# Key/value weights in two transfers, and another order for the first tiles of a cross-attention and expert layer

## The chip, the cores and the metric

One core of a Trainium2 chip runs the whole kernel. The metric is the device time of one execution in microseconds, the median of several; lower is better. The engines are PE (TensorE, the matrix engine; PEld is its weight load), DVE (VectorE), ACT (ScalarE), POOL (GpSimd) and SP (SyncE, which here only issues transfers).

## The reference

The input `x` is (16, 64, 512): 1024 tokens of width 512. `ctx` has the same shape. One block of cross attention with 32 query heads and 8 key/value heads of width 16, then a gated low-rank expert layer:

```python
x = x + _L0_xattn_ref(_layernorm(x), ctx_4096, ctx_4096, itok_BxS2_0_2047, Wq, Wk, Wv, Wo)
x = x + _L0_ffn_ref(_layernorm(x), A_w, B_w, Wq_w, keys)
...
q, k, v = heads(query @ Wq), heads(key @ Wk), heads(value @ Wv)
q = q * cos + _rotate_half(q) * sin
k = k * cos + _rotate_half(k) * sin
probs = softmax(q @ k.T * scale)
out = (probs @ v) @ Wo
...
scores = (x @ Wq_w.T) @ keys.T
top_vals, top_idx = top_k(scores, 16)
gate = one_hot(top_idx) weighted by softmax(top_vals)
out = ((x @ A_w.T) * gate) @ B_w.T * SCALING
```

## The kernel before

The 1024 tokens are cut into 8 tiles of 128 (two batches of 64 each). Every engine has a program of its own, written out by hand: a function `first()`, a function `second()`, then `step(i)` for i from 1 to 5, and `last()`. Semaphores with counts order the engines against each other. No scheduler decides anything: the order of the work on an engine is the order of the calls.

Products are made in reduced-precision pairs. A float32 operand `w` is split into a high part `w_hi` (ACT, `split_hi`, a rounded copy) and a low part `w_lo` (`split_lo`, `w - w_hi`); a product is then hi*hi + hi*lo + lo*hi. In the listing `high_part` makes the first two and `low_part` the third. The first tiles are an exception: `raw_kv(0)`, `raw_kv(1)` and `raw_q(0)` multiply the float32 operands as they are, since the split weights are not ready then.

What the change touches lies in the first 25 us:

- **SP** issues the loads, first tile 0 of `x`, then `wkv` (the key and value weights, 512 KB), the four quarters of `wq`, and so on. ACT issues tile 0 of the context (`cT_in`, 256 KB) from its own queue.
- **PE** begins with `keep_warm`: 11 products of zeros (`WARM`), started as soon as DVE has cleared their operand. Then come `raw_kv(0, [0, 1])`, the transposes of the normalised tile 0 (`turn_xh(0)`), `raw_kv(0, [2, 3])`, four `raw_q(0, k)`, `raw_kv(1)`, `turn_xh(1)`, `turn_q(0)` (transposes of the rotated queries of tile 0), four small products of the router weights (`ROUTE`), the first half of tile 1's query projection, `scores(0, b)`, `turn_k(1)`, the other half of the projection, `turn_xh(2)`, `kv_high(2)`, `turn_m(0)`, `kv_low(2)`, and then `second()`, which begins with `turned_scores(0)`.
- **ACT** rounds the weights (`wkv_hi`, `wq_hi`), copies the transposed tile 0 (`xT_raw`), makes the sine and cosine tables `cs`, normalises tile 1 (`xh`, `normalise(1)`) and rounds the transposed results (`xT_hi`, `qT_hi`).
- **POOL** makes the low parts `wkv_lo` and `wq_lo` (line L311), and the standard deviations: `deviation1(t)` writes `rstd` and `shift`, which ACT's `normalise(t)` waits for.
- **DVE** rotates queries and keys, makes the low parts `xT_lo`, `qT_lo`, `kT_lo` of what comes out of PSUM, and the maxima of the scores (`top`, line L856), from which `m_parts` makes `m_split` for `turn_m`. In `attend(t)` it normalises the attention's output, which ACT rounds (`oT_hi`) for PE's `out_high(t)`.

`scores(0, 0)` waits for `qT_hi`, `qT_lo`, the blocks of keys and the router's copy; `turn_xh(1)` waits for `xh`; `turn_m(0)` waits for `m_split`.

Of the kernel before, what the change touches and what calls it, by code (L numbers as in the profile page):

```python
# [15 lines left out]
DK = D // P  # L16
# [27 lines left out]
WARM = 11  # L44
# [10 lines left out]
def build(nc, x, xT, cT, pos, wq, wqT, wkv, wo, aT, router, bT, out):  # L55
    ctx = ExitStack()
    with ctx:
# [6 lines left out]
        def sem(name):  # L64
            return ctx.enter_context(nc.semaphore(name))
# [136 lines left out]
        ld_wkv = sem("ld_wkv")  # L202
# [7 lines left out]
        wq_h, wq_l, wkv_h, wkv_l = sem("wq_h"), sem("wq_l"), sem("wkv_h"), sem("wkv_l")  # L210
# [27 lines left out]
        def _(sp):  # L238
# [29 lines left out]
            sp.dma_start(wkv_sb[:], wkv).then_inc(ld_wkv, 16)  # L268
# [39 lines left out]
        def _(pool):  # L308
            def split_lo(lo, raw, hi, high, low, k):
                pool.wait_ge(high, k + 1)  # L310
                pool.tensor_tensor(lo[:, k, :], raw[:, k, :], hi[:, k, :].bitcast(F32),  # L311
                                   ALU.subtract).then_inc(low, 1)
# [95 lines left out]
            def first():  # L408
                deviation1(0)
                pool.wait_ge(rope_step, 9)  # L410
                for k in range(DK):
                    split_lo(wkv_lo, wkv_sb, wkv_hi, wkv_h, wkv_l, k)
                split_lo(wq_lo, wq_sb, wq_hi, wq_h, wq_l, 0)
                deviation1(1)
                split_lo(wq_lo, wq_sb, wq_hi, wq_h, wq_l, 1)
                k_blocks(0, 0)
                k_blocks(0, 1)
                split_lo(wq_lo, wq_sb, wq_hi, wq_h, wq_l, 2)
                split_lo(wq_lo, wq_sb, wq_hi, wq_h, wq_l, 3)
# [61 lines left out]
        def _(act):  # L481
# [145 lines left out]
            def first():  # L627
                act.wait_ge(const_ok, J + 1)
                act.activation(preload[:, 0:1], half_pi[:], ACT.Sin)
                act.wait_ge(ld_wkv, 16)  # L630
                for k in range(DK):
                    split_hi(wkv_hi, wkv_sb, wkv_h, k)
# [137 lines left out]
        def _(dve):  # L770
# [220 lines left out]
            def first():  # L991
# [38 lines left out]
                                pick_sum[:].unsqueeze(3).broadcast_to([P, 2, 2, BATCH])).then_inc(sel_ok, 1)  # L1030
                dve.wait_ge(cs_ok, 4)
                rotate_k(0)
                statistics1(1)
                k_low(0)
# [4 lines left out]
                                  table(HD, 0, H), ALU.mult).then_inc(q_rot, 1)  # L1039
                dve.wait_ge(q_rot, 1)  # L1040
# [94 lines left out]
        def _(pe):  # L1135
# [33 lines left out]
            def kv_high(t):  # L1169
                if t == RAW:  # L1170
                    pe.wait_ge(wkv_l, DK)
                    pe.wait_ge(v_st_ok, t)
                pe.wait_ge(c_hi_ok, t - RAW + 1)
                high_part(ps_w1[:, 0:2 * KV], chunk(cT_hi), wkv_hi, wkv_lo, slice(0, 2 * KV))
# [161 lines left out]
            def first():  # L1336
# [3 lines left out]
                pe.wait_ge(ld_wkv, 16)  # L1340
                raw_kv(0, [0, 1])
                turn_xh(0)
                raw_kv(0, [2, 3]).then_inc(kv_ps, 1)
                for k in range(DK):
                    pe.wait_ge(ld_wq[k], 16)
                    mm = raw_q(0, k)
                    if k == 2:
                        turn_k(0)
                mm.then_inc(q_ps, 1)
                raw_kv(1).then_inc(kv_ps, 1)  # L1350
                pe.wait_ge(kT_lo_ok, 1)
                turn_xh(1)
                turn_q(0)
# [4 lines left out]
                mm.then_inc(route_ps, 1)  # L1358
                q_high_part(1, [0, 1])
                q_low_part(1, [0, 1])  # L1360
# [3 lines left out]
                turn_k(1)  # L1364
                project_q(1, [2, 3]).then_inc(q_ps, 1)
                pe.wait_ge(qT_lo_ok, 1)
                turn_xh(2)
                kv_high(2)
                turn_m(0)
                kv_low(2)  # L1370

            def second():
                pe.wait_ge(sel_ok, 2)
                turned_scores(0)
                pe.wait_ge(q_rot, 4)
# [177 lines left out]
```

## Time and profile before

| | |
|---|---|
| median of 3 runs | 171.19 us (170.63 to 171.31) |
| the profiled execution | 170.7 us |
| its span on the core | 169.0 us |
| PE busy | 163.9 us, 97% |
| DVE busy | 132.8 us, 79% |
| ACT, POOL busy | 90.1 us, 91.8 us |

The span runs from the first to the last recorded instruction; the 1.7 us beside it are the launch and the end. Positions below are microseconds from the span's start. A busy time on PE contains the stretches in which one product drains while the next is fed, so consecutive rows of PE overlap; what a piece of work costs PE is the distance between the starts of its first row and of the next piece's.

### The profile page before, as it was taken

What the parts mean: (1) busy time and instruction counts of PE and PEld (TensorE: products, weight loads), DVE (VectorE), ACT (ScalarE), POOL (GpSimd) and SP (SyncE); (2) the same over time, 40 slices, a digit from 0 to 9 for tenths busy, and PEclk for the clock granted to TensorE, in tenths of its full rate; (3) what the DMA queues carried; (4) which work ended last, traced back from release to release, by engine and by line L of the source; (5) the groups of instructions that cost most, each with busy time, mean ns of one, the idle gap of its engine ahead of it and who ended that gap; (6) DMA issues with size and microseconds to landing.
All of it is one profiled execution on the core that took longest, in us unless ns stands there. A gap on an engine that the chain in (4) does not pass through costs nothing.

```text
span 169.0 us, 4082 instructions
## 1 busy us (share of the span) xinstructions
PE 163.9 (97%) x1439; PEld 130.2 (77%) x1439; DVE 132.8 (79%) x393; ACT 90.1 (53%) x212; POOL 91.8 (54%) x114
## 2 busy tenths in 40 slices
PE   7999999999999999999999999999999999999993
PEld 2647786777878787888879787888879776889883
DVE  2849896996998899669995799669985988767752
ACT  3397889899656462733635462733338154333210
POOL 5489989999899654830493354930450303512100
PEclk9999999999999999999999999999999999999999
DMA  5899980403203020301003000100001001000013
GB/s 170 306 418 385 407 260 10 124 31 100 66 0 124 4 62 0 113 16 62 6 0 124 0 4 0 62 6 0 4 0 62 4 0 62 8 0 0 0 62 124
DMA packets 6595, 13.46 MB, mean 80 GB/s; under 512 B 816, under 2 KB 1200, under 8 KB 6320
## 3 DMA queue, kind: packets, MB, share of 16 engines
q1 hardware_dynamic: 6288, 12.95, 21.9%
q8 instruction: 11, 0.18, 0.5%
q10 hardware_dynamic: 288, 0.27, 0.5%
q14 instruction: 8, 0.07, 0.1%
HBM read 11.11 MB, written 2.10 MB: 78 GB/s over the span
## 4 chain that ended last, share of the span: by engine, by line
PE 83%; DVE 7%; ACT 6%; issue 2%; ACTq 0%; DVEq 0%
PE ps_w L1145 14%; PE ps_w L1146 13%; PE ps_w L1150 12%; PE ps_t L1158 7%; PE ps_s L1230 6%; PE ps_s L1266 5%; PE ps_s L1249 4%; PE ps_w L1138 3%; PE ps_w L1140 3%; PE ps_t L1163 3%; PE ps_w L1139 3%; ACT eT L567 2%; PE ps_s L1146 2%; PE ps_s L1150 2%; PE ps_s L1145 2%
## 5 line engine op out<-in xcount | busy, mean ns | idle before, releaser
L364 POOL TENSOR_TENSOR oT_lo<-o_n,oT_hi 128x512 fp32r<-128x512 f32 x8 | 10.3, 1289 | 27.0 <-ACT oT_hi L575 26.9
L856 DVE TENSOR_REDUCE ps_s<-ps_s 128x8 f32<-128x512 f32 x32 | 21.0, 691 | 0.8 <-PE ps_s L1230 0.6
L567 ACT ACTIVATE eT<-ps_s 128x512 f32<-128x512 f32 x32 | 17.0, 600 | 4.6 <-PE ps_s L1255 4.5
L379 POOL TENSOR_TENSOR late<-late,gate 128x512 f32<-128x512 f32 x7 | 7.6, 1080 | 15.2 <-DVE gate L949 15.2
L1145 PE MATMUL ps_w<-am_hi,x2T_hi 128*128 128x288 f32 x48 | 14.0, 313 | 0.0
L355 POOL TENSOR_TENSOR k_bd_lo<-kT_lo,half_mask 128x512 fp32r<-128x512 f32 x8 | 8.3, 1041 | 10.3 <-DVE kT_lo L820 10.3
L1146 PE MATMUL ps_w<-am_lo,x2T_hi 128*128 128x288 f32 x48 | 13.1, 295 | 0.0
L874 DVE STREAM_TRANSPOSE o_s<-ps_s 128x1024 f32<-128x1024 f32 x8 | 10.0, 1244 | 2.2 <-PE ps_s L1266 2.2
L1145 PE MATMUL ps_w<-wo_hi,oT_hi 128*128 128x512 f32 x28 | 11.3, 404 | 0.3 <-ACT oT_hi L575 0.3
L1138 PE MATMUL ps_w<-wq_hi,xT_hi 128*128 128x512 f32 x26 | 11.2, 429 | 0.0
L575 ACT ACTIVATE oT_hi<-o_n 128x512 fp32r<-128x512 f32 x8 | 5.1, 631 | 11.4 <-DVE o_n L889 11.4
L1146 PE MATMUL ps_w<-wo_lo,oT_hi 128*128 128x512 f32 x28 | 11.0, 394 | 0.0
L1145 PE MATMUL ps_w<-b_hi,zT_hi 128*128 128x512 f32 (+1 forms) x28 | 10.8, 390 | 0.0
L1145 PEld LDWEIGHTS ps_w<-am_hi,x2T_hi 128*128 128x128 f32 x48 | 9.0, 188 | 1.9 <-ACT late L599 0.5
L560 ACT ACTIVATE mT<-ps_s 128x256 fp32r<-128x256 f32 x8 | 3.1, 383 | 13.8 <-PE ps_s L1239 13.8
L1146 PE MATMUL ps_w<-b_lo,zT_hi 128*128 128x512 f32 (+1 forms) x28 | 10.4, 377 | 0.0
L917 DVE TENSOR_TENSOR x2T_lo<-ps_t,x2T_hi 128x512 fp32r<-128x512 f32 x7 | 4.8, 690 | 7.0 <-ACT x2T_hi L588 7.0
L1140 PE MATMUL ps_w<-wq_hi,xT_lo 128*128 128x512 f32 x26 | 10.3, 394 | 0.0
L1139 PE MATMUL ps_w<-wq_lo,xT_hi 128*128 128x512 f32 x26 | 10.2, 392 | 0.0
L1230 PE MATMUL ps_s<-k_bd_hi,qT_hi 64*128 64x256 f32 x64 | 10.1, 310 | 0.0
L345 POOL TENSOR_TENSOR q_r<-q_a,q_b 128x512 f32<-128x512 f32 x7 | 9.1, 1297 | 0.5 <-DVE q_b L839 0.5
L1230 PE MATMUL ps_s<-k_bd_hi,qT_lo 64*128 64x256 f32 x64 | 9.2, 279 | 0.0
(236 smaller groups left out, 530.4 us busy)
## 6 DMA issues: line engine op xcount, KB each, us to landing
x_sb<-x SPq DMA_DIRECT2D x8, 256.0 KB, 7.1
cT_in<-cT SPq DMA_DIRECT2D x7, 256.0 KB, 3.3
out<-res SPq DMA_DIRECT2D x7, 256.0 KB, 2.0
wq_sb<-wq SPq DMA_DIRECT2D x4, 256.0 KB, 6.5
late<-wo SPq DMA_DIRECT2D x1, 1024.0 KB, 9.0
am_sb<-aT SPq DMA_DIRECT2D x1, 1024.0 KB, 8.7
b_sb<-bT SPq DMA_DIRECT2D x1, 1024.0 KB, 7.1
xT_raw<-xT SPq DMA_DIRECT2D x4, 256.0 KB, 3.0
```

The costliest lines, as they stand in the source:

```text
L364: pool.tensor_tensor(oT_lo[:], o_n[:].rearrange("p (b r q) -> p r b q", b=2, r=REP), oT_hi[:].bitcast(F32), ALU.subtract).then_inc(oT_lo_o ...
L567: act.activation(eT[:, c].rearrange("p b n -> p (b n)"), ps_s[:, c, :], ACT.Exp)\
L856: dve.tensor_reduce(neg_top[:, b, HALF_H * half:HALF_H * (half + 1), :], ps_s[:, 2 * (1 - b) + half, :].rearrange("p (r h k) -> p h r k", ...
L874: dve.transpose(o_s[:].rearrange("p h u g d -> p (h u g d)"), ps_o.rearrange("p h n -> p (h n)")).then_inc(o_step, 1)
L1138: pe.matmul(dst, hi(k), w_hi[:, k, cols], start=(k == 0), stop=False)
L1139: pe.matmul(dst, hi(k), w_lo[:, k, cols], start=False, stop=False)
L1140: mm = pe.matmul(dst, lo(k), w_hi[:, k, cols], start=False, stop=(k == DK - 1))
L1145: pe.matmul(dst, hi(k), w_hi[:, k, cols], start=(k == 0), stop=False)
L1146: pe.matmul(dst, hi(k), w_lo[:, k, cols], start=False, stop=False)
L1150: mm = pe.matmul(dst, lo(k), w_hi[:, k, cols], start=False, stop=(k == DK - 1))
L1158: mm = pe.transpose(dst[:, P * k:P * (k + 1)], src[:, P * k:P * (k + 1)], ident[:])
L1230: mm = pe.matmul(ps_s[:, 2 * (1 - b) + half, 2 * P * rp:2 * P * (rp + 1)], q[rows, t % 2, b, 2 * rp:2 * rp + 2, :].rearrange("p r q -> p ( ...
```

## The change

`wkv` is loaded in two transfers of 256 KB, each with its semaphore, and PE begins `raw_kv(0, [0, 1])` when the first half is there. `WARM` goes from 11 to 9. The low parts of the last two quarters of `wkv` are made by DVE and no longer by POOL. On PE `turn_k(0)`, `turn_q(0)`, `q_low_part(1)`, `turn_m(0)` and `kv_low(2)` move; on DVE `k_low(0)` moves behind the first half of the rotation of tile 0's queries; on POOL the second quarter of `wq_lo` moves ahead of `deviation1(1)`.

```diff
@@ -41,7 +41,7 @@
 SCALE = float(HD) ** -0.5
 GATE_SCALE = 32 / TOP
 STEPS = 12
-WARM = 11
+WARM = 9
 TAKEN = -3.0e38
 MAGIC = 1.5 * 2.0 ** 23
 TWO_PI = 2 * np.pi
@@ -199,7 +199,7 @@
         ld_c = [sem(f"ld_c{t}") for t in range(T)]
         ld_wq = [sem(f"ld_wq{k}") for k in range(DK)]
         ld_xT = {t: sem(f"ld_xT{t}") for t in range(DIRECT, T)}
-        ld_wkv = sem("ld_wkv")
+        ld_wkv = [sem(f"ld_wkv{half}") for half in range(2)]
         wq_sum_ok, sums_ps, sums_ok = (sem(n) for n in ("wq_sum_ok", "sums_ps", "sums_ok"))
         ld_wqT = [sem(f"ld_wqT{k}") for k in range(DK)]
         cs_q_ok, q_mean_ok = sem("cs_q_ok"), sem("q_mean_ok")
@@ -207,7 +207,7 @@
         sel_ok, const_ok, mask_step = sem("sel_ok"), sem("const_ok"), sem("mask_step")
         v_ones = sem("v_ones")
         rope_step, cs_ok = sem("rope_step"), sem("cs_ok")
-        wq_h, wq_l, wkv_h, wkv_l = sem("wq_h"), sem("wq_l"), sem("wkv_h"), sem("wkv_l")
+        wq_h, wq_l, wkv_h, wkv_l, wkv_l_late = (sem(n) for n in ("wq_h", "wq_l", "wkv_h", "wkv_l", "wkv_l_late"))
         wo_h, wo_l, am_h, am_l, b_h, b_l = (sem(n) for n in ("wo_h", "wo_l", "am_h", "am_l", "b_h", "b_l"))
         route_ps, route_ok = sem("route_ps"), sem("route_ok")
         stat1, rstd1_ok, shift1_ok = sem("stat1"), sem("rstd1_ok"), sem("shift1_ok")
@@ -265,7 +265,9 @@
                 sp.dma_start(out[t], res[:]).then_inc(stored, 16)
 
             load_x(0)
-            sp.dma_start(wkv_sb[:], wkv).then_inc(ld_wkv, 16)
+            for half in range(2):
+                ks = slice(2 * half, 2 * half + 2)
+                sp.dma_start(wkv_sb[:, ks, :], wkv[:, ks, :]).then_inc(ld_wkv[half], 16)
             for k in range(DK):
                 sp.dma_start(wq_sb[:, k, :], wq[:, k, :]).then_inc(ld_wq[k], 16)
             load_x(1)
@@ -408,11 +410,11 @@
             def first():
                 deviation1(0)
                 pool.wait_ge(rope_step, 9)
-                for k in range(DK):
+                for k in range(2):
                     split_lo(wkv_lo, wkv_sb, wkv_hi, wkv_h, wkv_l, k)
                 split_lo(wq_lo, wq_sb, wq_hi, wq_h, wq_l, 0)
+                split_lo(wq_lo, wq_sb, wq_hi, wq_h, wq_l, 1)
                 deviation1(1)
-                split_lo(wq_lo, wq_sb, wq_hi, wq_h, wq_l, 1)
                 k_blocks(0, 0)
                 k_blocks(0, 1)
                 split_lo(wq_lo, wq_sb, wq_hi, wq_h, wq_l, 2)
@@ -627,8 +629,8 @@
             def first():
                 act.wait_ge(const_ok, J + 1)
                 act.activation(preload[:, 0:1], half_pi[:], ACT.Sin)
-                act.wait_ge(ld_wkv, 16)
                 for k in range(DK):
+                    act.wait_ge(ld_wkv[k // 2], 16)
                     split_hi(wkv_hi, wkv_sb, wkv_h, k)
                 x_raw(0)
                 act.wait_ge(rope_step, 9)
@@ -1028,15 +1030,17 @@
                 dve.wait_ge(sel_ok, 1)
                 dve.tensor_copy(sel[:].rearrange("p b (h k) -> p b h k", h=2),
                                 pick_sum[:].unsqueeze(3).broadcast_to([P, 2, 2, BATCH])).then_inc(sel_ok, 1)
+                split_lo(wkv_lo, wkv_sb, wkv_hi, wkv_h, wkv_l_late, 2)
+                split_lo(wkv_lo, wkv_sb, wkv_hi, wkv_h, wkv_l_late, 3)
                 dve.wait_ge(cs_ok, 4)
                 rotate_k(0)
                 statistics1(1)
-                k_low(0)
                 dve.wait_ge(q_ps, 1)
                 H = REP * KVH
                 w = ps_w0[:].rearrange("p (h s j) -> p h s j", h=H, s=2)
                 dve.tensor_tensor(q_b[:].rearrange("p (h s j) -> p h s j", h=H, s=2), w[:, :, ::-1, :],
                                   table(HD, 0, H), ALU.mult).then_inc(q_rot, 1)
+                k_low(0)
                 dve.wait_ge(q_rot, 1)
                 dve.tensor_tensor(w, w, table(0, 0, H), ALU.mult).then_inc(q_rot, 1)
                 dve.wait_ge(q_rot, 2)
@@ -1168,7 +1172,8 @@
 
             def kv_high(t):
                 if t == RAW:
-                    pe.wait_ge(wkv_l, DK)
+                    pe.wait_ge(wkv_l, 2)
+                    pe.wait_ge(wkv_l_late, 2)
                     pe.wait_ge(v_st_ok, t)
                 pe.wait_ge(c_hi_ok, t - RAW + 1)
                 high_part(ps_w1[:, 0:2 * KV], chunk(cT_hi), wkv_hi, wkv_lo, slice(0, 2 * KV))
@@ -1337,41 +1342,41 @@
                 pe.wait_ge(warm_ok, 1)
                 keep_warm(ps_t1[:], WARM)
                 pe.wait_ge(ident_ok, 1)
-                pe.wait_ge(ld_wkv, 16)
+                pe.wait_ge(ld_wkv[0], 16)
                 raw_kv(0, [0, 1])
                 turn_xh(0)
+                pe.wait_ge(ld_wkv[1], 16)
                 raw_kv(0, [2, 3]).then_inc(kv_ps, 1)
                 for k in range(DK):
                     pe.wait_ge(ld_wq[k], 16)
                     mm = raw_q(0, k)
-                    if k == 2:
-                        turn_k(0)
                 mm.then_inc(q_ps, 1)
+                turn_k(0)
                 raw_kv(1).then_inc(kv_ps, 1)
                 pe.wait_ge(kT_lo_ok, 1)
                 turn_xh(1)
-                turn_q(0)
                 pe.wait_ge(ld_router, 16)
                 for k in range(DK):
                     rows = slice(QUAD * k, QUAD * (k + 1))
                     mm = pe.matmul(ROUTE[:, k, :], router_sb[rows, 0:P], router_sb[rows, P:P + E], start=True, stop=True)
                 mm.then_inc(route_ps, 1)
+                turn_q(0)
                 q_high_part(1, [0, 1])
-                q_low_part(1, [0, 1])
                 pe.wait_ge(route_ok, 1)
                 scores(0, 0)
                 scores(0, 1)
                 turn_k(1)
+                q_low_part(1, [0, 1])
                 project_q(1, [2, 3]).then_inc(q_ps, 1)
                 pe.wait_ge(qT_lo_ok, 1)
                 turn_xh(2)
+                turn_m(0)
                 kv_high(2)
-                turn_m(0)
-                kv_low(2)
 
             def second():
                 pe.wait_ge(sel_ok, 2)
                 turned_scores(0)
+                kv_low(2)
                 pe.wait_ge(q_rot, 4)
                 project_q(2, [0, 1])
                 turn_q(1)
```

PE, from the raw query products of tile 0 (`wq_sb,xT_raw`) to the query projection of tile 1 (`wq_hi`, `wq_lo`; `eT` holds the router weights here). Before:

```order
L1334 MATMUL ps_w<-wq_sb,xT_raw 128x512 x3
L1186 MATMUL ps_t<-ident,k_r 128x128
L1334 MATMUL ps_w<-wq_sb,xT_raw 128x512
L1328 MATMUL ps_w<-wkv_sb,cT_in 128x256 x4
L1158 MATMUL ps_t<-ident,xh 128x128 x4
L1158 MATMUL ps_t<-ident,q_r 128x128 x4
L1357 MATMUL ps_s<-eT 128x64 x4
L1145 MATMUL ps_w<-wq_hi,xT_hi 128x512
L1146 MATMUL ps_w<-wq_lo,xT_hi 128x512
L1145 MATMUL ps_w<-wq_hi,xT_hi 128x512
L1146 MATMUL ps_w<-wq_lo,xT_hi 128x512
L1150 MATMUL ps_w<-wq_hi,xT_lo 128x512 x2
```

And in the changed kernel (its lines are numbered 4 or 5 higher):

```order
L1339 MATMUL ps_w<-wq_sb,xT_raw 128x512 x4
L1191 MATMUL ps_t<-ident,k_r 128x128
L1333 MATMUL ps_w<-wkv_sb,cT_in 128x256 x4
L1162 MATMUL ps_t<-ident,xh 128x128 x4
L1361 MATMUL ps_s<-eT 128x64 x4
L1162 MATMUL ps_t<-ident,q_r 128x128 x4
L1149 MATMUL ps_w<-wq_hi,xT_hi 128x512
L1150 MATMUL ps_w<-wq_lo,xT_hi 128x512
L1149 MATMUL ps_w<-wq_hi,xT_hi 128x512
L1150 MATMUL ps_w<-wq_lo,xT_hi 128x512
L1235 MATMUL ps_s<-k_bd_hi,qT_hi 128x256 x2
```

The transpose of the rotated keys (`k_r`) has gone from the midst of the query products to behind them, the router's products ahead of the transposes of `q_r`, and the row with `xT_lo` no longer stands ahead of the scores.

PE, around the transposes of the maxima (`m_split`) of tile 0. Before, the last products of `kv_high(2)` and `kv_low(2)` stand on both sides of them:

```order
L1146 MATMUL ps_w<-wkv_lo,cT_hi 128x256
L1145 MATMUL ps_w<-wkv_hi,cT_hi 128x256
L1146 MATMUL ps_w<-wkv_lo,cT_hi 128x256
L1239 MATMUL ps_s<-ident,m_split 128x128 x2
L1150 MATMUL ps_w<-wkv_hi,cT_lo 128x256 x4
L1249 MATMUL ps_s<-qT_hi,k_bd_hi 128x256 x4
L1249 MATMUL ps_s<-qT_hi,k_bd_lo 128x256 x4
L1249 MATMUL ps_s<-qT_lo,k_bd_hi 128x256 x4
```

In the changed kernel the transposes follow `turn_xh(2)` at once:

```order
L1144 MATMUL ps_w<-wq_hi,xT_lo 128x512
L1162 MATMUL ps_t<-ident,xh 128x128 x4
L1244 MATMUL ps_s<-ident,m_split 128x128 x2
L1149 MATMUL ps_w<-wkv_hi,cT_hi 128x256
L1150 MATMUL ps_w<-wkv_lo,cT_hi 128x256
```

and `kv_low(2)` (the row with `cT_lo`) stands behind the whole of `turned_scores(0)`:

```order
L1254 MATMUL ps_s<-qT_hi,k_bd_lo 128x256 x4
L1254 MATMUL ps_s<-qT_lo,k_bd_hi 128x256 x4
L1260 MATMUL ps_s<-mT,sel 128x256 x4
L1154 MATMUL ps_w<-wkv_hi,cT_lo 128x256 x4
L1142 MATMUL ps_w<-wq_hi,xT_hi 128x512
```

So the maxima are wanted eight products earlier, and the four of `kv_low(2)` come later.

POOL, from `deviation1(0)` to the first block of keys. Before:

```order
L320 TENSOR_TENSOR rstd<-ve,neg_half 128x1
L311 TENSOR_TENSOR wkv_lo<-wkv_sb,wkv_hi 128x256 x4
L311 TENSOR_TENSOR wq_lo<-wq_sb,wq_hi 128x512
L320 TENSOR_TENSOR rstd<-ve,neg_half 128x1
L327 TENSOR_SCALAR shift<-mv,rstd 128x1
L311 TENSOR_TENSOR wq_lo<-wq_sb,wq_hi 128x512
L355 TENSOR_TENSOR k_bd_hi<-kT_hi,half_mask 128x512
```

And in the changed kernel:

```order
L322 TENSOR_TENSOR rstd<-ve,neg_half 128x1
L313 TENSOR_TENSOR wkv_lo<-wkv_sb,wkv_hi 128x256 x2
L313 TENSOR_TENSOR wq_lo<-wq_sb,wq_hi 128x512 x2
L322 TENSOR_TENSOR rstd<-ve,neg_half 128x1
L329 TENSOR_SCALAR shift<-mv,rstd 128x1
L357 TENSOR_TENSOR k_bd_hi<-kT_hi,half_mask 128x512
L357 TENSOR_TENSOR k_bd_lo<-kT_lo,half_mask 128x512
```

Two of the four `wkv_lo` are gone, and both `wq_lo` stand ahead of `rstd` and `shift` of tile 1.

## Rows read from the trace of the kernel before

**Rows 1.** The page of the kernel before: busy shares, and the chain by engine.
```profile
PE 163.9 (97%) x1439; PEld 130.2 (77%) x1439; DVE 132.8 (79%) x393; ACT 90.1 (53%) x212; POOL 91.8 (54%) x114
...
PE 83%; DVE 7%; ACT 6%; issue 2%; ACTq 0%; DVEq 0%
```

**Rows 2.** Busy time by stretch; columns PE, PEld, DVE, ACT, POOL, clock, DMA, GB/s.
```profile
1.24:6.00 4.76, 4.76 (x11) 1.51 (x12) 2.24 (x10) 1.83 (x4) 2.35 (x12) 1.00 0.80 260
6.00:7.53 1.53, 1.53 (x5) 1.25 (x5) 1.39 (x7) 0.99 (x4) 0.52 (x1) 1.00 0.82 270
...
7.97:8.91 0.94, 0.94 (x6) 0.60 (x5) 0.00 (x0) 0.74 (x3) 0.94 (x2) 1.00 1.05 405
31.71:47.93 16.22, 16.06 (x150) 12.21 (x150) 14.07 (x34) 13.65 (x36) 15.05 (x14) 1.00 0.28 77
```

**Rows 3.** DMA issues of the first 6 us: KB each, us from issue to landing.
```profile
wkv_sb<-wkv SPq DMA_DIRECT2D x1, 512.0 KB, 4.4
cT_in<-cT ACTq DMA_DIRECT2D x1, 256.0 KB, 4.6
```

**Rows 4.** When the two transfers were issued: start us, us, queue, line.
```profile
1.22 0.46 ACTq L483 DMA_DIRECT2D cT_in<-cT  x1
...
1.24 0.42 SPq L268 DMA_DIRECT2D wkv_sb<-wkv  x1
```

**Rows 5.** POOL's timeline: start us, us, line, tiles, [idle before, releaser].
```profile
7.01 2.83 POOL L311 TENSOR_TENSOR wkv_lo<-wkv_sb,wkv_hi 128x256 fp32r<-128x256 f32 x4 [1.64 <-ACT wkv_hi L486]
10.13 1.28 POOL L311 TENSOR_TENSOR wq_lo<-wq_sb,wq_hi 128x512 fp32r<-128x512 f32 x1 [0.29 <-ACT wq_hi L486]
11.74 0.56 POOL L320 TENSOR_TENSOR rstd<-ve,neg_half 128x1 f32<-128x1 f32 x1 [0.33 <-DVE ve L787]
12.40 0.27 POOL L327 TENSOR_SCALAR shift<-mv,rstd 128x1 f32<-128x1 f32 x1
```

**Rows 6.** ACT's timeline.
```profile
12.85 0.80 ACT L498 ACTIVATE xh<-x_sb,shift,rstd 128x512 f32<-128x512 f32 x1
...
14.89 0.60 ACT L509 ACTIVATE xT_hi<-ps_t 128x512 fp32r<-128x512 f32 x1 [0.72 <-PE ps_t L1158]
15.63 0.60 ACT L552 ACTIVATE qT_hi<-ps_t 128x512 fp32r<-128x512 f32 x1
```

**Rows 7.** PE's timeline.
```profile
14.26 0.60 PE L1158 MATMUL ps_t<-ident,xh 128*128 128x128 f32 x4
14.94 0.66 PE L1158 MATMUL ps_t<-ident,q_r 128*128 128x128 f32 x4
...
15.90 0.51 PE L1145 MATMUL ps_w<-wq_hi,xT_hi 128*128 128x512 f32 x1
...
17.51 0.39 PE L1230 MATMUL ps_s<-k_bd_hi,qT_hi 64*128 64x256 f32 x2
...
19.12 0.33 PE L1186 MATMUL ps_t<-ident,k_r 128*128 128x128 f32 x1
...
20.68 0.60 PE L1158 MATMUL ps_t<-ident,xh 128*128 128x128 f32 x4
...
25.66 0.60 PE L1158 MATMUL ps_t<-ident,q_r 128*128 128x128 f32 x4
...
31.71 0.47 PE L1145 MATMUL ps_w<-wo_hi,oT_hi 128*128 128x512 f32 x1 [0.33 <-ACT oT_hi L575]
```

**Rows 8.** DVE's timeline.
```profile
9.56 0.30 DVE L807 TENSOR_TENSOR ps_w<-ps_w,cs 128x128 f32<-128x128 f32 x1 [1.67 <-ACT cs L638]
...
16.26 0.69 DVE L844 TENSOR_TENSOR qT_lo<-ps_t,qT_hi 128x512 fp32r<-128x512 f32 x1
...
18.52 2.63 DVE L856 TENSOR_REDUCE ps_s<-ps_s 128x8 f32<-128x512 f32 x4 [0.57 <-PE ps_s L1230]
...
21.51 0.29 DVE L868 TENSOR_TENSOR m_split<-ps_s,m_split 128x128 fp32r<-128x128 f32 x1
...
26.98 0.69 DVE L844 TENSOR_TENSOR qT_lo<-ps_t,qT_hi 128x512 fp32r<-128x512 f32 x1 [1.46 <-ACT qT_hi L552]
```

## The prediction, made before the changed kernel had run

> **What bounds the kernel now.** I read the page first. PE is busy for 97% of the span, and the chain that ended last lies on PE for 83% [rows 1]. So only two kinds of change can move the time: work taken off PE, and waits of PE taken away or added. The change removes two products of zeros and no useful product, so everything goes by waits. The windows show where they are: from 31.71 to 47.93 PE is busy for 16.06 of 16.22 us [rows 2], and it stays like that up to the last stages. What counts is therefore how early PE reaches 31.71 us. Its timeline names what held it there: `out_high(0)` waited 0.33 us for `oT_hi` [rows 7], the end of `attend(0)` on DVE, and DVE begins that chain with `qT_lo` of tile 1 at 26.98, after 1.46 us idle for `qT_hi` [rows 8], which needs PE's `turn_q(1)` at 25.66 [rows 7]. So `turn_q(1)` is the point to follow: if it moves by d, everything behind it moves by d. PE does the same useful work before it in both kernels. Only its start, its waits and its clock differ.
>
> **The start.** Eleven products of zeros end near 6.0 [rows 2], 0.43 us each. The first product needs context tile 0, which lands at 1.22 + 4.6 = 5.8, and `wkv`, at 1.24 + 4.4 = 5.6 [rows 3, 4]. With nine, PE is free at about 5.1. The halved load has 256 KB less in front of or beside the context; at the 380 GB/s or so that the engines move when full (405 in one window [rows 2]) that is 0.65 us, a landing at 5.15, and with at most the 0.2 us from landing to product that the trace has, a start at 5.4. The bounds are 5.1 (free PE) and 6.0 (nothing gained). I take 5.4: 0.6 us earlier.
>
> Half of that is lost to the clock. The first two chunks took 1.53 us, the last two, the same work, 0.94 [rows 2]. The zeros, 512 columns in 0.43 us, ran at the level of 1.2 GHz, the last two chunks at 2.4; wholly at the lower level the first two would take twice 0.94, less the short wait in it, 1.8. So the clock rose near 7.2, inside the first product, though the profile's clock column prints 1.00 throughout. Begun at 5.4, that product runs at the lower level to its end: 5.4 + 1.8 = 7.2 against 7.53. The gain is **-0.3 us**.
>
> The second half of `wkv` lands where the whole did, about 5.7 to 5.9, and is wanted at 7.7: at nothing. ACT rounds those quarters 0.3 us later than now and waits for `xh`'s transposes anyway.
>
> **To the transposes of tile 1.** From 8.91 to 14.26 PE works without a wait: 5.35 us. From 8.6 that ends at 13.95. But `xh` of tile 1 is late now. POOL starts the first `wq_lo` at 10.13, when ACT has rounded its quarter, and took the rest in the order `rstd`, `shift`, `wq_lo` [rows 5]. ACT's rounding follows PE, so 9.83. Now both `wq_lo` come first: 9.83 + 2 x 1.28 = 12.35; `rstd` and `shift` took 12.67 - 11.74 = 0.93, so `shift` is ready at 13.3 instead of 12.67. ACT starts `xh` at 13.3, not 12.85, and takes 0.80 [rows 6]: PE can start at 14.12. That is **+0.15 us** of waiting. The two `wkv_lo` taken off POOL (0.71 each [rows 5]) help nothing, because POOL then waits for ACT's `wq_hi`: it would have been idle.
>
> On DVE the two `wkv_lo` cost between 0.30 (128x128) and 0.69 us (128x512) each [rows 8]: 0.6 to 1.4 in the 1.67 us in which DVE waited for the tables `cs` [rows 8]. At nothing; if that cover went, at most the excess over 1.67 would reach `rotate_k(0)`.
>
> **To the scores.** In the trace the four transposes (0.44, from 7.53 to 7.97 [rows 2]) ended at 14.70 and `turn_q(0)` began at 14.94 [rows 7]: 0.24 us wait for `q_r`. In the new order the router's products, about 0.4 of the 0.96 from 14.94 to 15.90 [rows 7], fill it: 14.12 + 0.44 + 0.4 = 14.96. The wait goes, **-0.24**, but `turn_q(0)` is where it was. So `qT_hi` (15.63 [rows 6]) and `qT_lo` (16.26 + 0.69 = 16.95 [rows 8]) are where they were. `k_low(0)`, about 0.3 us, now stands inside the rotation, but the query product ends 0.4 earlier (start, and `turn_k` behind it): `q_r` is ready at 14.7, under cover of the router.
>
> The scores need `qT_lo`: 17.0 at the earliest. The six products from 15.90 to 17.51 took 1.61 us [rows 7], the two low ones a third, 0.54. PE starts the four at 15.5 and is done at 16.6. `q_low_part`, which now covers that time, stands behind the scores. So PE waits **+0.4 us** for DVE. That is where the reordering gives back what it won: PE reaches the scores 0.5 us earlier and has 0.54 us of work still to do.
>
> **To `turn_q(1)`.** Scores 17.0 to 18.6 (1.61, from 17.51 to 19.12), then `turn_k(1)`, the low part and the rest, 1.56 + 0.54 [rows 7]: `turn_xh(2)` at 20.7, as now (20.68). Then comes `turn_m(0)`, at 21.15 if free. DVE begins `top` 1.01 us after the scores began (18.52 - 17.51) and has `m_split` 3.28 later (21.51 + 0.29 - 18.52 [rows 8]): 17.0 + 1.0 + 3.3 = 21.3. Before, `kv_high(2)` stood in front and covered this. **+0.15 to 0.2 us**. Behind it the same products come in another order up to `turn_q(1)`; I take 0.1 us off for a short wait on `mT` and a change of operand kind that the order saves (an estimate; the trace has both at about 0.1).
>
> **The sum at `turn_q(1)`:** -0.3 + 0.15 - 0.24 + 0.4 + 0.2 - 0.1 = +0.1 us. The values of tile 0 and the projection behind start some tenths earlier or later, but PE then waits longer at 31.71 for the same DVE chain. The rest costs nothing: the fifth context load waits for `kv_low(2)`, which ends a good microsecond later, but its buffer is read many microseconds on; SP's one issue more (0.42 us [rows 4]) delays transfers that the full DMA engines (share 1.05 [rows 2]) would have held back anyway. So 170.7 + 0.1 = 170.8 in terms of the profiled execution, which lies 0.5 us under the median of the runs shown, 171.2. **Predicted: 171.3 us.** A measurement of this kernel tells about 0.5%, 0.86 us, from no change.
>
> **A rule against the change.** 256 KB and 512 KB both move at about the full rate here [rows 2, 3], so splitting costs no bandwidth. "DMA: Bandwidth & Descriptors" of the Trainium skill, "Rules for kernel authors", says that two transfers of disjoint halves are not worth it, since they use the same engines, and wants 1 MiB in each. Its example is halves by partition; taken over, it is the first rival.
>
> **Rivals.**
>
> 1. *The split gains nothing*: context tile 0 still lands at 5.8, the product starts at 6.0, PE idles 0.9 us behind the nine products. For it: the same bytes go through the same engines. Against it: half of `wkv` moves behind the context. The -0.3 goes: 171.2 + 0.4 = 171.6. Chance 0.13.
> 2. *The waits don't come*: `qT_lo` or `m_split` is ready sooner, because DVE and ACT gain the 0.3 of the start too. Without the 0.4 and 0.2, 170.7. If in addition the clock rises before the first product in most executions, its start gives the whole 0.6 and `xh` follows: 171.3 - 0.6 - 0.3 = 170.4, and a few tenths more would be faster by over 0.5%. Chances 0.12 and 0.06.
> 3. *The clock rises late, slower*: PE is now idle from 5.1 to 5.4, shortly ahead of the point at which the clock rose, where it had been busy since 1.24. If the rise then took as long from 5.4 as it took from 1.24, it would come at 11.4; 4.2 us of work at half the clock cost 2.1 us, of which the waits for `xh` and `qT_lo` absorb some 0.4: 173.0. It decides (0.86 us over 171.2) if the rise is later than about 9.5. Against it: 0.3 us is short beside the 3.9 us of work ahead of it and the products behind it. Chance 0.09. "TensorE: Matmul & The Clock Gate" of the Trainium skill, "What's actually happening", says that the throttled state is the default, that activity releases it, and that the point varies from run to run; no run here shows yet what a short gap does.
>
> **How the numbers follow.** The forecast has 0.60; it spans 170.9 to 171.7, by 0.3 to 0.4 either way for the landing and the clock. The two cases near it inside 0.5% have 0.25. Same: 0.85. Faster: 0.06. Slower: 0.09. The range takes in rivals 1 and the first of 2 and the spread of the runs shown (0.7 us): 170.5 to 172.0.
>
> **What would show each step.** PE's first product at 5.3 to 5.5 and its first transposes near 7.2. DVE's `wkv_lo` near 0.4 us each, done before `cs`. ACT's `xh` of tile 1 at 13.3. `turn_q(0)` within 0.15 of 14.94, and no wait before it. A wait of PE of 0.3 to 0.5 us for `qT_lo` before the scores, and one of 0.1 to 0.3 for `m_split`. `turn_q(1)` at 25.6 to 25.9, `out_high(0)` at 31.7 to 31.9, with a wait for `oT_hi`. The prediction is wrong if DVE's chain from `qT_lo` of tile 1 starts more than 0.5 us off 26.98, or if a wait appears behind 31.9 that is not there now.

## The result, and the profile after

| | before | changed |
|---|---|---|
| median, 22 runs each | 170.66 us (170.14 to 171.76) | 171.63 us (171.22 to 172.66) |
| ratio to before, 95% interval | | 1.0048 (1.0034 to 1.0063) |
| the profiled execution | 170.7 us | 171.9 us |
| its span | 169.0 us | 170.0 us |

The change costs 0.5%, about 0.8 us by the ratio (the medians differ by 0.97). The forecast of 171.3 us (no change that can be told) lies 0.3 us beside the median, and its range holds it; but against the kernel before it forecast +0.1 us, and 0.8 came.

The windows of the changed kernel, columns as in [rows 2]:

```profile
4.20:5.10 0.90, 0.90 (x3) 0.15 (x1) 0.83 (x6) 0.03 (x1) 0.23 (x1) 1.00 1.07 403
5.10:6.90 1.80, 1.68 (x9) 1.39 (x9) 1.63 (x8) 1.42 (x4) 0.34 (x1) 1.00 0.64 146
6.90:8.70 1.80, 1.10 (x7) 0.64 (x4) 1.77 (x4) 1.36 (x5) 1.45 (x2) 1.00 0.95 303
8.70:12.00 3.30, 2.88 (x7) 1.43 (x8) 1.34 (x6) 2.82 (x5) 2.19 (x2) 1.00 1.08 421
```

The same windows of the kernel before:

```profile
5.10:6.90 1.80, 1.80 (x5) 0.94 (x4) 1.63 (x9) 1.24 (x4) 0.27 (x1) 1.00 0.75 199
6.90:8.70 1.80, 1.80 (x11) 1.46 (x9) 0.95 (x3) 0.62 (x3) 1.69 (x3) 1.00 1.01 388
```

The last two columns are the DMA engines' share and GB/s. Both kernels have a hole from 5.1 to 6.9, just where the quarters of `wq` begin; the rate falls to 199 GB/s before and to 146 now, and it lasts longer now: 303 GB/s against 388 in the next window. That is (199 - 146) x 1.8 + (388 - 303) x 1.8 = 250 KB less by 8.7 us, 0.6 us at the 400 GB/s around it. Tile 1 of `x` comes 1.25 us late (below), twice that; what makes up the rest, no view here shows.

The DMA issues of the first 4.5 us (KB each, us to landing; the median where there are several). The context lands earlier than in [rows 3]. So does the first half of `wkv`, at 1.24 + 3.8 = 5.0 us; the second, issued at 1.7, takes 4.1 and lands at 5.8, no earlier than the whole did (5.6). `wq` takes longer (6.5 before), and was issued 0.5 us later too:

```profile
wq_sb<-wq SPq DMA_DIRECT2D x4, 256.0 KB, 7.2
x_sb<-x SPq DMA_DIRECT2D x2, 256.0 KB, 5.3
wkv_sb<-wkv SPq DMA_DIRECT2D x2, 256.0 KB, 3.9
cT_in<-cT ACTq DMA_DIRECT2D x1, 256.0 KB, 4.0
```

PE's timeline of the changed kernel, which answers to [rows 7]:

```profile
5.39 1.31 PE L1333 MATMUL ps_w<-wkv_sb,cT_in 128*128 128x256 f32 x4
6.53 0.60 PE L1162 MATMUL ps_t<-ident,xh 128*128 128x128 f32 x4
6.97 1.03 PE L1333 MATMUL ps_w<-wkv_sb,cT_in 128*128 128x256 f32 x4
9.12 3.70 PE L1339 MATMUL ps_w<-wq_sb,xT_raw 128*128 128x512 f32 x8 [1.12 <-DMA wq_sb<-wq]
...
14.90 0.63 PE L1162 MATMUL ps_t<-ident,xh 128*128 128x128 f32 x4 [0.25 <-ACT xh L500]
15.46 0.45 PE L1361 MATMUL ps_s<-eT 32*128 32x64 f32 x8
15.84 0.66 PE L1162 MATMUL ps_t<-ident,q_r 128*128 128x128 f32 x4
...
18.11 0.38 PE L1235 MATMUL ps_s<-k_bd_hi,qT_hi 64*128 64x256 f32 x2 [0.68 <-DVE qT_lo L846]
...
21.76 0.60 PE L1162 MATMUL ps_t<-ident,xh 128*128 128x128 f32 x4
22.47 0.44 PE L1244 MATMUL ps_s<-ident,m_split 128*128 128x128 f32 x2
...
26.90 0.60 PE L1162 MATMUL ps_t<-ident,q_r 128*128 128x128 f32 x4
...
32.77 0.47 PE L1149 MATMUL ps_w<-wo_hi,oT_hi 128*128 128x512 f32 x1 [0.43 <-ACT oT_hi L577]
```

The start is what was forecast, and better: the first product at 5.39, the transposes already at 6.53. PE would be free for `raw_q` at 7.91 (6.97 plus the 0.94 of [rows 2]), a whole microsecond ahead of the 8.91 of before. Then it waits until 9.12 for the first quarter of `wq`. The second late load is tile 1 of `x`, on the chain of DVE, POOL and ACT:

```profile
11.81 0.69 DVE L780 BATCH_NORM_STATS2 bn<-x_sb 128x6 f32<-128x512 f32 x1 [1.93 <-DMA x_sb<-x]
9.81 2.50 POOL L313 TENSOR_TENSOR wq_lo<-wq_sb,wq_hi 128x512 fp32r<-128x512 f32 x2 [1.27 <-ACT wq_hi L488]
12.99 0.56 POOL L322 TENSOR_TENSOR rstd<-ve,neg_half 128x1 f32<-128x1 f32 x1 [0.69 <-DVE ve L789]
13.65 0.27 POOL L329 TENSOR_SCALAR shift<-mv,rstd 128x1 f32<-128x1 f32 x1
13.95 0.81 ACT L500 ACTIVATE xh<-x_sb,shift,rstd 128x512 f32<-128x512 f32 x1 [0.18 <-POOL shift L329]
```

Before, the same statistics began at 10.56; now at 11.81. POOL has both `wq_lo` done by 12.31 and then waits 0.69 us for DVE's `ve`, so it is not POOL's order that makes `xh` late, but the load. `xh` moves from 12.85 [rows 6] to 13.95. Of that, 0.64 us are left at `turn_xh(1)` (14.26 to 14.90) and 0.60 at the scores. `turn_q(1)` comes 1.24 us later [rows 7]: to the 0.6 of the scores is added the work that the new order still owes behind them, and a wait for `m_split`. `out_high(0)` then comes 1.06 later, the turning of the sums 1.05 (47.93 to 48.98), the span is 1.0 longer.

### The profile page after: what moved, and what is told of

It is laid out like the page before. It is cut to its first block, busy times and chain, and to the rows that moved or that the text cites. A ratio compares the mean times of both kernels' runs of the same rounds, so it can differ in the third digit from the quotient of the medians.

```text
span 170.0 us, 4081 instructions
## 1 busy us (share of the span) xinstructions
PE 163.0 (96%) x1437; PEld 129.6 (76%) x1437; DVE 133.8 (79%) x395; ACT 90.7 (53%) x212; POOL 90.4 (53%) x112
## 4 chain that ended last, share of the span: by engine, by line
PE 77%; DVE 9%; DMA 5%; ACT 3%; issue 2%; SPq 2%; POOL 0%; ACTq 0%; DVEq 0%
PE ps_w L1149 14%; PE ps_w L1154 12%; PE ps_w L1150 12%; PE ps_t L1162 7%; PE ps_s L1235 6%; DMA x_sb<-x 5%; PE ps_s L1254 4%; PE ps_s L1271 4%; PE ps_w L1142 3%; PE ps_w L1144 3%; PE ps_w L1143 3%; DVE ps_s L858 3%; PE ps_s L1150 2%; PE ps_s L1154 2%; PE ps_s L1149 2%
## 5 line engine op out<-in xcount | busy, mean ns | idle before, releaser
L1235 PE MATMUL ps_s<-k_bd_lo,qT_hi 64*128 64x256 f32 x64 | 9.3, 279 | 0.0
```

Of the source, the lines that this page charges most:

```text
L1235: mm = pe.matmul(ps_s[:, 2 * (1 - b) + half, 2 * P * rp:2 * P * (rp + 1)], q[rows, t % 2, b, 2 * rp:2 * rp + 2, :].rearrange("p r q -> p ( ...
```

## The experiments

All ratios are to the kernel before, timed on the same chip in the same job (its median there was 170.7, 171.1 and 171.05 us in the three jobs). The diffs show the lines that carry the edit; the waits and declarations that follow from it are left out. First, which part of the change costs.

**The changed kernel with `wkv` in one transfer** (order, nine zero products and DVE's low parts kept):

```diff
-            for half in range(2):
-                ks = slice(2 * half, 2 * half + 2)
-                sp.dma_start(wkv_sb[:, ks, :], wkv[:, ks, :]).then_inc(ld_wkv[half], 16)
+            sp.dma_start(wkv_sb[:], wkv).then_inc(ld_wkv, 16)
```

> The changed kernel with one change back: wkv comes in one transfer again, and the first product waits for all of it. Theory 1 (the extra transfer delays what is queued behind it): the first quarter of wq lands at about 7.7 us instead of 9.07, tile 1 of x at 10.5 instead of 11.8, PE's wait of 1.12 us before the raw query products goes although the first product starts at 6.0 instead of 5.39, and the time falls by 0.4 to 0.7 us against the changed kernel, to some 0.2% over the kernel before. Theory 2 (the transfers are harmless, the new order costs it all): the landings stay late or do not matter, the later first product costs 0.3 us more, ratio to before 1.006 or above.

Measured: median 171.15 us, ratio 1.0051 (1.0021 to 1.0081). The twelve times fall into two groups: seven from 170.8 to 171.2, five from 172.2 to 172.7. The profiled execution (170.85 us) is of the first; its timelines of PE and DVE:

```profile
6.09 1.10 PE L1331 MATMUL ps_w<-wkv_sb,cT_in 128*128 128x256 f32 x4 [1.19 <-DMA cT_in<-cT]
...
10.59 0.69 DVE L778 BATCH_NORM_STATS2 bn<-x_sb 128x6 f32<-128x512 f32 x1 [0.65 <-DMA x_sb<-x]
...
14.95 0.66 PE L1160 MATMUL ps_t<-ident,q_r 128*128 128x128 f32 x4
17.22 0.39 PE L1233 MATMUL ps_s<-k_bd_hi,qT_hi 64*128 64x256 f32 x2 [0.69 <-DVE qT_lo L844]
...
21.57 0.44 PE L1242 MATMUL ps_s<-ident,m_split 128*128 128x128 f32 x2
25.99 0.60 PE L1160 MATMUL ps_t<-ident,q_r 128*128 128x128 f32 x4
```

The loads are back at their old times (statistics at 10.59, before 10.56), and the positions are those of the sum to 0.3 us: `turn_q(0)` 14.95 (forecast 14.96), the scores 17.22 (17.0), `turn_m` 21.57 (21.3), `turn_q(1)` 25.99 (25.6 to 25.9). That they fit so well is in part luck: the first product starts at 6.09, not at the 5.4 of the sum, and makes it up because it runs at the faster clock from its start (0.94 us to the transposes, at 7.03). Where loads are not late, the lower group is some 0.2 us above the kernel before, as the prediction worked out for the order. By the ratio over all twelve times, this kernel is not told from the changed one (1.0048); that the loads recover is read from its trace and from the lower group. The second group is taken up below.

**The kernel before with the split alone** (two transfers, two waits, the old order, eleven zero products):

```diff
-            sp.dma_start(wkv_sb[:], wkv).then_inc(ld_wkv, 16)
+            for half in range(2):
+                ks = slice(2 * half, 2 * half + 2)
+                sp.dma_start(wkv_sb[:, ks, :], wkv[:, ks, :]).then_inc(ld_wkv[half], 16)
...
+                pe.wait_ge(ld_wkv[1], 16)
                 raw_kv(0, [2, 3]).then_inc(kv_ps, 1)
```

> The kernel before with the split load alone: two transfers, ACT and PE wait for each half, WARM 11, every order as before. Theory 1: landings behind the split are late by about 1.3 us on the last engine, DVE waits for tile 1 of x until 11.8, and the time rises by 0.3 to 0.7 us (ratio 1.002 to 1.004). Theory 2: landings as in the kernel before, ratio 0.998 to 1.001.

Measured: median 171.63 us over seven times, ratio 1.0061 (1.0036 to 1.0086), dearer than the 1.002 to 1.004 that was expected. The whole cost is here, and nothing else of the change is in it. Its `out_high(0)` comes at 32.62, 0.91 us later than before, where the changed kernel's comes 1.06 later. Its window from 5.1 to 6.9 has the same hole:

```profile
5.10:6.90 1.80, 1.80 (x6) 1.26 (x5) 1.63 (x9) 1.37 (x4) 0.29 (x1) 1.00 0.62 137
```

and its timelines of PE and DVE the same two late loads:

```profile
9.13 0.70 PE L1336 MATMUL ps_w<-wq_sb,xT_raw 128*128 128x512 f32 x1 [0.40 <-DMA wq_sb<-wq]
...
11.84 0.69 DVE L780 BATCH_NORM_STATS2 bn<-x_sb 128x6 f32<-128x512 f32 x1 [1.73 <-DMA x_sb<-x]
```

**Two edits of the new order taken back in the changed kernel**: POOL's second `wq_lo` behind `deviation1(1)` again, and `q_low_part(1)` ahead of the scores again.

```diff
                 split_lo(wq_lo, wq_sb, wq_hi, wq_h, wq_l, 0)
-                split_lo(wq_lo, wq_sb, wq_hi, wq_h, wq_l, 1)
                 deviation1(1)
+                split_lo(wq_lo, wq_sb, wq_hi, wq_h, wq_l, 1)
```

> The changed kernel with POOL's order back: rstd and shift of tile 1 ahead of the second quarter of wq_lo. By the prediction's step this gives back 0.15 us of PE's wait for xh. Theory 1 says that in the changed kernel the late tile 1 of x holds rstd at 12.99 after both wq_lo are done, so that the order changes nothing there or makes it worse (the second wq_lo then comes behind shift, at 13.9): same time, ratio to before 1.004 to 1.006. Theory 2: 0.15 to 0.4 us faster than the changed kernel, ratio 1.002 to 1.004.

```diff
                 q_high_part(1, [0, 1])
+                q_low_part(1, [0, 1])
                 pe.wait_ge(route_ok, 1)
                 scores(0, 0)
                 scores(0, 1)
                 turn_k(1)
-                q_low_part(1, [0, 1])
```

> The changed kernel with q_low_part(1) ahead of the scores of tile 0 again. The wait of 0.68 us for qT_lo is filled with 0.5 us of products. If the wait is a loss by itself (prediction's step, 0.4 us): 0.3 to 0.5 us faster, ratio 1.001 to 1.003. If the chain through qT_lo, the scores and the maxima is what counts, turn_q(1) moves little because the products save their time behind the scores and PE still waits for m_split there: under 0.2 us faster, ratio 1.003 to 1.005.

Measured: 1.0059 (1.0040 to 1.0079) and 1.0055 (1.0033 to 1.0077). Neither gives anything back. With POOL's old order, POOL waited 1.87 us for `ve`: the order had nothing to win while the statistics were late. With the low part first, `turn_q(1)` came at 26.79 instead of 26.90: the 0.54 us of work filled the 0.68 of waiting (0.22 was left), but the late DVE chain from `qT_lo` is what the next stage waits for, and PE then stood 0.57 us for `m_split`. A step on which the sum put 0.15 us and one with 0.4 are thus not where the measured 0.8 comes from.

Next, what makes a split of the same bytes slow. `wkv` lies in memory as 128 rows of 4 KB and `wq` as 128 rows of 8 KB, so a half of `wkv` is 2 KB out of every 4, and a quarter of `wq` 2 KB out of every 8.

**The split alone, with each half contiguous in memory** (the values are laid out so beforehand):

```diff
-                sp.dma_start(wkv_sb[:, ks, :], wkv[:, ks, :]).then_inc(ld_wkv[half], 16)
+                sp.dma_start(wkv_sb[:, ks, :], wkv[half]).then_inc(ld_wkv[half], 16)
```

> The kernel before with the split load, and the host lays the two halves of wkv out one behind the other, so that each transfer reads one contiguous block of 256 KB instead of 2 KB pieces with gaps of 2 KB. Theory A (the gaps in what a transfer reads slow some engines): wq's first quarter lands at 7.7 at the last engine, x tile 1 at 10.6, ratio 0.997 to 1.000. Theory B (the number of transfers or of pieces does it, wherever they lie): landings at 9.0 and 11.8 as with the split alone, ratio 1.004 to 1.007.

Measured: 1.0023 (1.0001 to 1.0045). In 5.1 to 6.9 us 217 GB/s instead of 137; PE starts `raw_q` at 7.88, but waits for the second quarter until 9.20, and the statistics start at 11.23. That lies between the two theories. By the ratios more than half of the cost is gone, though the intervals overlap; the hole is not gone, but no longer deeper than in the kernel before (199 GB/s).

**The kernel before, with the quarters of `wq` contiguous**, `wkv` in one transfer:

```diff
-                sp.dma_start(wq_sb[:, k, :], wq[:, k, :]).then_inc(ld_wq[k], 16)
+                sp.dma_start(wq_sb[:, k, :], wq[k]).then_inc(ld_wq[k], 16)
...
-        "wq": rows(np.asarray(L0_xattn_Wq)),
+        "wq": rows(np.asarray(L0_xattn_Wq)).transpose(1, 0, 2),
```

> The kernel before with one edit: the host lays wq out so that each quarter is one contiguous block; before, each quarter reads 2 KB pieces at a distance of 8 KB. Theory A: the stretch from 5.1 to 6.8 us in which the DMA engines are not full goes, wq's first quarter lands 0.3 to 0.6 us earlier than 7.67, x tile 1 0.3 to 0.6 earlier than 10.54, and since PE does not wait for either in the kernel before, the time falls by 0.2 us at most. Theory B: landings within 0.15 us of the kernel before, same time.

Measured: median 170.11 us, ratio 0.9941 (0.9919 to 0.9964): faster than before, by 1.0 us. The hole, which the kernel before has too, is gone from its window:

```profile
5.10:6.90 1.80, 1.32 (x7) 1.00 (x7) 1.63 (x9) 1.34 (x4) 0.29 (x1) 1.00 1.05 395
```

and in its timelines of PE and DVE both readers start about 0.8 us earlier:

```profile
1.24 4.06 PE L1163 MATMUL ps_t<-warm 128*128 128x512 bf16 x11 [1.24 <-DVE warm L992]
5.78 1.10 PE L1328 MATMUL ps_w<-wkv_sb,cT_in 128*128 128x256 f32 x4 [0.48 <-DMA cT_in<-cT]
6.72 0.60 PE L1158 MATMUL ps_t<-ident,xh 128*128 128x128 f32 x4
8.10 1.96 PE L1334 MATMUL ps_w<-wq_sb,xT_raw 128*128 128x512 f32 x4
...
9.70 0.69 DVE L778 BATCH_NORM_STATS2 bn<-x_sb 128x6 f32<-128x512 f32 x1
```

So the hole belongs to the strided reads of `wq`, and strided halves of `wkv` ahead of them make it deeper. It was a surprise that the kernel before gains more than the 0.2 us expected at most: its rows name no wait of PE for `wq`. And the 0.81 us at `raw_q` is not a wait for `wq` that went. The first product starts 0.22 us earlier (5.78 against 6.00), and from there to the transposes takes 0.94 us instead of 1.53, because the clock rose earlier: the eleven zero products took 4.06 us. Before:

```profile
1.24 4.87 PE L1163 MATMUL ps_t<-warm 128*128 128x512 bf16 x11 [1.24 <-DVE warm L992]
6.00 1.69 PE L1328 MATMUL ps_w<-wkv_sb,cT_in 128*128 128x256 f32 x4
```

The two together are the 0.81. The load's own share in this trace is smaller: `xh` of the kernel before, done at 12.85 + 0.80 = 13.65, would have held a `turn_xh(1)` that came at 13.45 by 0.2 us (an estimate from these rows). The gain itself is not chance: the spans of all ten executions are 168.1 to 168.6 us, those of the kernel before in the same job 168.7 to 169.7. But whether the layout also brings the clock's rise forward, or by what other way it gains the rest, one profiled execution of each does not tell.

**The kernel before, with `wkv` in two transfers by partitions**, 64 each, which is the case of the rule that the prediction cites:

```diff
-            sp.dma_start(wkv_sb[:], wkv).then_inc(ld_wkv, 16)
+            for half in range(2):
+                ps = slice(ROWS * half, ROWS * (half + 1))
+                sp.dma_start(wkv_sb[ps], wkv[ps]).then_inc(ld_wkv, 16)
```

> The kernel before with wkv in two transfers again, but cut by partitions (64 each): the pieces stay 4 KB, each transfer is contiguous, and all wait for both. Theory B1 (one transfer more ahead of wq is what delays): wq at 9.0, x tile 1 at 11.8, ratio 1.003 to 1.007. Theory B2 (smaller pieces do it) and theory A: landings within 0.2 us of 7.67 and 10.54, ratio 0.998 to 1.002.

Measured: 1.0059 (1.0019 to 1.0100). The halves take 5.1 us from issue to landing instead of 4.4 for the whole, the engines moved 205 GB/s from 4.2 to 5.1 us (387 before), and the first product starts at 7.62. "DMA: Bandwidth & Descriptors" of the Trainium skill, "Rules for kernel authors", says that such halves serialize; that alone would leave the end of the second where the whole's was (5.6). Here the first half landed at 5.8 and the second at 7.5, so the trace is worse than the rule.

**The kernel before, with `wkv` in one transfer of 2 KB pieces** (more and smaller descriptors, no second transfer):

```diff
-            sp.dma_start(wkv_sb[:], wkv).then_inc(ld_wkv, 16)
+            sp.dma_start(wkv_sb[:].rearrange("p (h k) n -> p h (k n)", h=2),
+                         wkv.rearrange("h p k n -> p h (k n)")).then_inc(ld_wkv, 16)
```

> The kernel before with wkv in one transfer, but of 2 KB pieces (256 of them, each half contiguous in DRAM). Theory B2 (twice as many pieces ahead of wq): wq at 8.5 to 9.1, x tile 1 at 11.2 to 11.8, ratio 1.002 to 1.006. Theories A and B1: landings within 0.2 us of the kernel before, except that context tile 0 may come up to 0.5 us earlier, ratio 0.997 to 1.001.

Measured: 0.9980 (0.9954 to 1.0006), the same as before; statistics at 10.66. The number of pieces of `wkv` is not the cost.

Last, the change under loads that are not late.

**The changed kernel with the quarters of `wq` and the halves of `wkv` contiguous** (both edits shown above):

> The changed kernel, with the quarters of wq and the halves of wkv laid out contiguously in memory, the same values and products. If the loads' stall is the larger part of the change's cost, wq's first quarter lands at 6.3 us instead of 9.1, tile 1 of x at 9.7 instead of 11.8, and turn_q(1) comes near 25 us: ratio to the kernel before 0.993 to 0.997. If the new order costs half a per cent by itself (the kernel with the whole load and the new order: 1.005), it shows in full now: turn_q(1) 0.5 us behind the kernel with contiguous wq (24.85), ratio 0.998 to 1.001. If the split costs for another reason, 1.003 or more.

**The same two layouts under the old order** (eleven zero products):

> The kernel before, with contiguous quarters of wq and wkv in two contiguous halves; the old order. If the split costs only by the stall of the engines on strided pieces, this is the kernel with contiguous wq again: first quarter of wq at 6.3 to 6.5 us, ratio 0.993 to 0.996, a few tenths better if the earlier first product counts. If the split costs by one issue more or by smaller pieces, 0.998 to 1.001.

**The changed kernel with contiguous quarters of `wq` only**, its strided halves kept:

> The changed kernel with contiguous quarters of wq and its two strided halves of wkv as they are. If only the strided reads of wq stall, it equals the kernel in which all is contiguous (within 0.2 per cent). If strided halves of wkv stall the engines by themselves, wq's first quarter lands 0.5 us or more later than in that one, and the ratio is higher by 0.3 per cent or more.

Measured, in that order: median 170.20 us, 0.9951 (0.9934 to 0.9969); 169.96 us, 0.9944 (0.9920 to 0.9968); 170.40 us, 0.9967 (0.9947 to 0.9986). All three are faster than the kernel before. With contiguous `wq` the two transfers of `wkv` cost nothing, and strided halves do not either within what can be told. It takes both, strided halves and strided quarters, for the full cost: in the third kernel the engines move 376 GB/s from 5.1 to 6.9 and the statistics start at 9.68. The timeline of PE in the first of them:

```profile
5.15 1.10 PE L1333 MATMUL ps_w<-wkv_sb,cT_in 128*128 128x256 f32 x4 [0.29 <-DMA cT_in<-cT]
7.69 2.38 PE L1339 MATMUL ps_w<-wq_sb,xT_raw 128*128 128x512 f32 x5
13.47 0.63 PE L1162 MATMUL ps_t<-ident,xh 128*128 128x128 f32 x4 [0.27 <-ACT xh L500]
16.69 0.39 PE L1235 MATMUL ps_s<-k_bd_hi,qT_hi 64*128 64x256 f32 x2 [0.70 <-DVE qT_lo L846]
25.46 0.60 PE L1162 MATMUL ps_t<-ident,q_r 128*128 128x128 f32 x4
```

and the second, the old order with the same loads:

```profile
5.43 1.03 PE L1330 MATMUL ps_w<-wkv_sb,cT_in 128*128 128x256 f32 x4
7.70 2.38 PE L1336 MATMUL ps_w<-wq_sb,xT_raw 128*128 128x512 f32 x5
13.05 0.61 PE L1160 MATMUL ps_t<-ident,xh 128*128 128x128 f32 x4
16.29 0.39 PE L1232 MATMUL ps_s<-k_bd_hi,qT_hi 64*128 64x256 f32 x2
24.64 0.60 PE L1160 MATMUL ps_t<-ident,q_r 128*128 128x128 f32 x4
```

Both start `raw_q` at 7.7. The new order then loses 0.42 us at `turn_xh(1)`, where it waits for `xh`; the scores come 0.40 later, with the 0.54 us of low part still owed, and `turn_q(1)` is 0.82 later. At the end 0.6 us of it is left in the spans of the profiled executions (168.5 and 167.9), but 0.1 in the medians of all spans (168.3 and 168.2) and 0.24 in those of the times. The intervals overlap, so by the times the two orders are not told apart; by the two traces the new one is the worse.

**The changed order, `wkv` whole, `wq` contiguous**:

> The changed kernel's order, with wkv in one transfer and contiguous quarters of wq: the order alone under loads that are not late. If the new order's waits (for qT_lo before the scores, for m_split) are what it costs, they stay at 0.4 to 0.7 and 0.2 us, and the ratio is 0.997 to 1.000 against 0.994 of the old order with the same loads. If the order costs nothing once wq is early, 0.993 to 0.995.

Measured: median 172.23 us, ratio 1.0040 (1.0008 to 1.0072), and again two groups, wider apart: four times from 170.5 to 170.8, eight from 172.1 to 172.6. The 0.997 to 1.000 expected for the order's waits is met by the lower group alone. In the profiled execution (170.82 us, of the lower group) PE stands idle for 1.40 us behind the nine zero products:

```profile
6.19 1.10 PE L1331 MATMUL ps_w<-wkv_sb,cT_in 128*128 128x256 f32 x4 [1.40 <-DMA cT_in<-cT]
```

The changed kernel, whose first product follows with almost no gap, has one time of 22 above 172.1, and the kernel with all loads contiguous (0.29 us idle) none of nine above 170.5. The three kernels with a long idle time there have an upper group: 1.19 us, five of twelve; 1.40 us, eight of twelve; and the split by partitions, 1.51 us, three of ten, at 173.2 to 173.8 against 171.3 to 171.9. This would be what rival 3 described: an idle stretch ahead of the rise of the clock puts the rise off in some executions. No profile was taken of an execution of an upper group, so that it is the clock is argued, not shown. The granted clock on record speaks for it in one kernel only: 0.99 in the three upper executions of the split by partitions against 0.999 to 1.0 in its others, but 0.999 to 1.0 in both groups of the other two. What is shown is that the upper groups came with the long idle stretch and, but for the one time of 22, with no short one.

## Why the prediction was right, and where its sum was not

- **The bound and the point to follow**: right. The delay at `turn_q(1)` (1.24 us) is carried on to 32.77, to the sums and to the end, less 0.2. But by the sign that the prediction set itself, it failed: DVE's `qT_lo` of tile 1 starts at 28.17, 1.19 us behind 26.98, where more than 0.5 was to count as wrong. The time came near, the position did not.
- **The start, -0.3 us**: the landing and the start (5.39 for 5.4) were right; the clock rose earlier than I took it, and the start brought PE 1.0 us by 7.91. The term was too small, and all of it was lost to the next.
- **The transfers behind the split, at nothing** (those "the full DMA engines would have held back anyway", and "splitting costs no bandwidth"): this is the step that was mis-sized. It took the engines to be full throughout the loads, from one window of 0.94 us in [rows 2]. Between 5.1 and 6.9 they are not full even before (share 0.75, 199 GB/s), and the window of 6.00 to 7.53 in [rows 2] already said 270 GB/s (share 0.82). Measured: the split alone costs 0.6% (1.0 us); the reader of `wq` that could start at 7.91 starts at 9.12, and that of tile 1 of `x` goes from 10.56 to 11.81.
- **`xh`, +0.15 us**: the mechanism (both `wq_lo` ahead of `rstd`) is seen only where loads are not late: 0.27 us of waiting in the kernel with both layouts contiguous. In the changed kernel the late tile covers it. At `turn_xh(1)` the sum had 14.12 and the trace 14.90: 0.78 of the missing 1.1 us are here.
- **`turn_q(0)` without a wait, `qT_lo` +0.4, `m_split` +0.15 to 0.2**: all there. The wait for `qT_lo` is 0.68, since PE resumes 0.25 us after DVE's row ends (17.17 + 0.69 = 17.86, 18.11), which the 0.4 left out. Before `turn_m`, PE is held from about 22.2 (21.76 plus 0.44) to 22.47, 0.27 us.
- **DVE's two `wkv_lo`, at nothing**: right in the effect, not in the size. They took 0.64 us each instead of about 0.4, and `rotate_k(0)` still began at 9.08, before the 9.56 of [rows 8].
- **Two slips of arithmetic** that change nothing: 9.83 + 2 x 1.28 is 12.39, not 12.35; and 256 KB cost 0.65 us at 405 GB/s, 0.69 at 380.
- **Rival 1** (the split gains nothing) had the price nearly right, 171.6, and the wrong mechanism: the first product did start earlier. The **rule** of the Trainium skill pointed the right way, for a reason that it does not give.
- **Rival 3** did not happen in the changed kernel, but is a possible cause of the upper groups above, which lie 1.6 to 1.9 us above the lower ones against the 1.7 worked out for it (173.0 against 171.3).

The order of tile 0 costs some tenths of a microsecond at most; the transfers cost the rest. The forecast time itself came close only because the median of three runs that it started from stood 0.5 us above that of 22: two errors of opposite sign.

## What to carry to other kernels

Read the DMA share in windows no longer than one transfer before calling the queues full, and price a split load by what is queued behind it, not by its own landing. If a weight is loaded in column blocks, try each block contiguous in memory first: here that was worth 0.6%, more than the reordering cost or gave, and it made the split harmless. Before a gain is put down to a load, look at when the clock rose in the two traces: here that alone made 0.59 us between two executions. When zero products that bridge a load are cut, time enough runs to see whether their end leaves PE idle: the median of a few can come out of either group.

## What the runs showed of the hardware

Reads of 2 KB out of every 8 KB (128 rows, 256 KB) stalled when they followed `wkv`: the engines moved 137 to 217 GB/s from 5.1 to 6.9 us, against 338 to 395 with the same bytes contiguous. From 6.9 to 8.7 us, with quarters of `wq` still in flight (in the kernel before the first lands at 7.7 and the last at 9.8), they moved 388 GB/s there and 303 in the changed kernel; why they stall just at first is open. "DMA: Bandwidth & Descriptors" of the Trainium skill, "Latency and other measured facts", reports for copies between tensors in HBM that the rate falls with the row pitch, from 207 GB/s at 512 KiB to 164 at 2 MiB and 103 at 4 MiB; a pitch of 8 KB is far below that, and no run here tells whether it is the same effect. Only contiguity was varied, not the pitch, so a padded layout was not tried.
